# Dense stage of a two-layer graph attention kernel: statistics two groups ahead, normalising and moving in turn on ScalarE, a PSUM wait per tile, edge table stored in 14 pieces

## The reference

```python
h = relu(layernorm(x))                       # per row: (x - mean) / sqrt(var + 1e-5)
for W, a_s, a_d, b in ((W0, ...), (W1, ...)):
    h = (h @ W).reshape(n, 4, 64)
    e = leaky_relu((h * a_s).sum(-1)[src] + (h * a_d).sum(-1)[dst], 0.2)   # with a loop on each node
    alpha = segment_softmax(e, dst)
    h = gelu(segment_sum(h[src] * alpha[:, :, None], dst).reshape(n, 256) + b)
out = x + h
```

## Time and profile before

| | us |
|---|---|
| median of 3 runs (4950.52, 4977.21, 4978.08) | 4977.21 |
| profiled execution, its own time | 4959.4 |
| its span in the trace | 4957.5 |
| first store of a dense group issued | 24.3 |
| last store of the dense stage issued | 166.8 |
| first gather of layer 0 | 169.8 |
| DVE begins the first step of layer 0 | 226.7 |
| POOL, PE, DVE, ACT busy over the span | 3054.6, 2920.6, 3692.9, 2353.5 |

### The profile page before, as it was taken

The page is one execution under the profiler, slowest core; times in us unless marked ns, Lnnn a source line. Parts: engine busy times, 40 slices in busy tenths (PEclk is TensorE's granted clock), DMA queues, the critical chain, the costliest instruction groups (busy, mean ns, idle before and its releaser), DMA issues.

```text
span 4957.5 us, 58322 instructions
## 1 busy us (share of the span) xinstructions
PE 2920.6 (59%) x10195; PEld 1927.3 (39%) x10195; DVE 3692.9 (74%) x13203; ACT 2353.5 (47%) x7376; POOL 3054.6 (62%) x3215
## 2 busy tenths in 40 slices
PE   7467666677666555565545555555555555555555
PEld 6244444444444333343423333333333333333333
DVE  7577777878777677676757777777777777777777
ACT  5255555555555444444443444444444444444445
POOL 7566656666656655566546666666666666666664
PEclk9688888888788777777767777777777777777777
DMA  8444444444444444444434444444444444444443
GB/s 266 141 129 128 128 119 128 132 128 126 125 120 127 124 115 123 117 121 122 122 99 124 128 133 133 133 133 132 133 135 133 132 130 133 133 133 131 134 135 91
DMA packets 326730, 645.75 MB, mean 130 GB/s; under 512 B 97683, under 2 KB 195387, under 8 KB 326635
## 3 DMA queue, kind: packets, MB, share of 16 engines
q0 software_dynamic: 152224, 428.76, 32.5%
q1 hardware_dynamic: 128664, 172.56, 11.5%
q10 hardware_dynamic: 45746, 43.56, 2.6%
HBM read 596.90 MB, written 47.71 MB: 130 GB/s over the span
## 4 chain that ended last, share of the span: by engine, by line
DVE 70%; issue 14%; another core or an unknown queue 11%; PE 2%; ACT 1%; DVEq 1%; POOL 1%; DMA 0%; ACTq 0%; SPq 0%; POOLq 0%
DVE rows_all L1081 9%; DVE groups_or_hots L1106 9%; DVE stores_or_hots L1059 5%; DVE of_node L1162 3%; DVE vectors_or_means L1201 3%; DVE total L1188 3%; DVE node_logit L1160 3%; DVE node_l L1152 2%; DVE runs L1117 2%; DVE dloc L1103 1%; DVE stats_or_carry L1122 1%; DVE runs L1119 1%; DVE logit L1180 1%; DVE pre L1178 1%
## 5 line engine op out<-in xcount | busy, mean ns | idle before, releaser
L598 POOL DMA_INDIRECT rows_all<-table,edge x3068 | 2933.2, 956 | 1821.5 <-issue 953.7
L1328 PE MATMUL bank<-rows_all,groups_or_hots 128*128 128x264 f32 x6272 | 1783.3, 440 | 47.3 <-issue 23.0
L1328 PEld LDWEIGHTS bank<-rows_all,groups_or_hots 128*128 128x128 f32 x6272 | 1328.9, 219 | 452.6 <-issue 147.2
L1310 PE MATMUL bank<-stores_or_hots,logit_p 128*128 128x448 bf16 x896 | 368.8, 566 | 1314.6 <-DVE logit_p L1072 1142.0
L706 ACT ACTIVATE rows_all<-rows_all 128x64 f32<-128x64 f32 x3584 | 881.6, 341 | 3.7
L1310 PEld LDWEIGHTS bank<-stores_or_hots,logit_p 128*128 128x128 bf16 x896 | 98.9, 131 | 1513.0 <-DVE logit_p L1072 1214.7
L1081 DVE TENSOR_TENSOR rows_all<-rows_all,bank 128x768 f32<-128x768 f32 (+1 forms) x672 | 658.8, 1037 | 0.0
L1106 DVE TENSOR_TENSOR groups_or_hots<-bank,dloc 128x1792 f32<-128x1792 f32 x224 | 453.5, 2025 | 159.5 <-remote 101.2
L736 ACT ACT_TABLE_LOAD x224 | 287.4, 1283 | 400.2 <-issue 377.6
L718 ACT ACTIVATE share<-node_d 128x8 f32<-128x8 f32 x224 | 47.0, 210 | 694.5 <-DVE node_d L1155 550.7
L730 ACT ACTIVATE bank<-fall 128x56 f32<-128x56 f32 x224 | 49.6, 222 | 544.2 <-DVE fall L1183 357.8
(11 more groups left out here) (192 smaller groups left out, 4054.9 us busy)
## 6 DMA issues: line engine op xcount, KB each, us to landing
normed_or_dst<-dst_row SPq DMA_DIRECT2D x224, 448.0 KB
rows_all<-table,edge POOLq DMA_INDIRECT x3068
products_or_rows<-table SPq DMA_DIRECT2D x224, 132.0 KB
table<-row ACTq DMA_DIRECT2D x112, 132.0 KB
early_or_lists<-in_x_dram SPq DMA_DIRECT2D x112, 128.0 KB
out_dram<-vectors_or_means ACTq DMA_DIRECT2D x112, 128.0 KB
table<-stores_or_hots ACTq DMA_DIRECT2D x24, 528.0 KB
groups_or_hots<-in_x_dram SPq DMA_DIRECT2D x24, 512.0 KB
```

Source lines behind the costliest of these rows:

```text
L598: nc.gpsimd.indirect_dma_start(out=G[u][:, j, :], out_offset=None, in_=table[L][0:N, :], in_offset=bass.IndirectOffsetOnAxis(ap=index[:, j ...
L1310: last = nc.tensor.matmul(bank[0][:, 0:SLOTS * SQ], logit_p[:, q * P:(q + 1) * P], of[:, q], start=(q == 0), stop=(q == QUADS - 1))
L1328: last = nc.tensor.matmul(bank[3 + t.half][:, 0:ROW], onehot[t.half][:, j, :], G[t.u][:, j, :], start=(j == 0), stop=(j == SLOTS - 1))
```

## The change

DVE: the turn is reordered. The scales of the next group come right behind copy 0, since its statistics were made a turn earlier; the statistics of the group after the next (`later`) are split, two tiles behind copy 0 and two behind copy 1, its sums behind copy 2, and the early tiles behind copies 2 and 3. The first turn makes two groups' statistics. ACT: `norm_group` and `move_rows` are split into tiles that go in turn, and the square root of `later` stands between moves 1 and 2. PE: for an even group it waits for one moved tile of the odd group before instead of four (the semaphore starts at 4 instead of 1 so that the waited value stays positive). POOL: 14 pieces of 640 columns, and so four early gathers behind each.

```diff
-        PIECE = 320
+        PIECE = 640
...
-            def norm_group(g):
+            def deviations(g):
                 m = len(g.sizes)
                 act.wait_ge(mv_done[g.b], g.n + 1)
                 nc.scalar.activation(sdev[g.b][:, 0:m], mv[g.b][:, 0:m, 1], ACT.Sqrt, bias=eps[:, 0:1]).then_inc(sdev_done[g.b], 1)
-                act.wait_ge(shift_done[g.b], g.n + 1)
...
+            def dense_turn(g, after, later):
+
+                norm_tile(after, 0)
+                norm_tile(after, 1)
+                move_tile(g, 0)
+                norm_tile(after, 2)
+                move_tile(g, 1)
+                norm_tile(after, 3)
+                if later:
+                    deviations(later)
+                move_tile(g, 2)
+                move_tile(g, 3)
+                store_group(g)
...
             for j in range(XB):
-                norm_group(Group(0, j + 1))
-                move_rows(Group(0, j))
-                store_group(Group(0, j))
+                dense_turn(Group(0, j), Group(0, j + 1), Group(0, j + 2))
...
-            def between(g, after, early=()):
+            def dense_turn(g, after, later, early=()):
 
                 copy_tile(g, 0)
-                stats_group(after)
+                scales_group(after)
+                if later:
+                    stats_tiles(later, 0, 2)
                 copy_tile(g, 1)
-                scales_group(after)
-                for t in range(2, GROUP):
-                    if early:
-                        early_tile(early[t - 2])
-                    copy_tile(g, t)
+                if later:
+                    stats_tiles(later, 2, GROUP)
+                copy_tile(g, 2)
+                if later:
+                    sums_group(later)
+                if early:
+                    early_tile(early[0])
+                copy_tile(g, 3)
+                if early:
+                    early_tile(early[1])
+
+            def first_turn(g, after, later):
+
+                copy_tile(g, 0)
+                stats_tiles(after, 0, GROUP)
+                sums_group(after)
+                copy_tile(g, 1)
+                scales_group(after)
+                copy_tile(g, 2)
+                stats_tiles(later, 0, GROUP)
+                copy_tile(g, 3)
+                sums_group(later)
...
                 if g.b == 0:
-                    pe.wait_ge(rows_copied[1], g.n * GROUP + 1)
+                    pe.wait_ge(rows_copied[1], g.n * GROUP + (t + 1 - GROUP + ODD_FIRST))
```

More of the change, by code:

```diff
@@ L298, in two_layer_graph_attention @@
         from_one = [normed, hnT_done, rows_done, hnT_copied, rows_copied]
+        ODD_FIRST = GROUP
+        rows_copied_0 = (1, ODD_FIRST)
         block = ctx.enter_context(nc.Block())
@@ L399, in _ @@
                 for each in one:
-                    nc.sync.sem_inc(each, 1)
+                    nc.sync.sem_inc(each, ODD_FIRST if each is rows_copied[1] else 1)
             load_group(Group(0, 0))
@@ L638, in move_rows, with norm_tile @@
-            def move_rows(g):
-                if not isinstance(g.n, int) or g.n > 0:
-                    act.wait_ge(rows_stored[g.b], g.n * 16)
-                for t, r in enumerate(g.sizes):
-                    act.wait_ge(rows_done[t % 2], g.n * GROUP + g.b * GROUP // 2 + t // 2 + 1 + 1)
-                    nc.scalar.activation(row0[g.b][0:r, t, :], bank[3 + t][0:r, 0:ROW], ACT.Identity).then_inc(rows_copied[g.b], 1)
+            def norm_tile(g, t):
+                if t >= len(g.sizes):
+                    return
+                r = g.sizes[t]
+                if t == 0:
+                    act.wait_ge(shift_done[g.b], g.n + 1)
+                    if not isinstance(g.q, int) or g.q > 1:
+                        for k in range(2):
+                            act.wait_ge(hnT_done[k], g.i * (XB // 2 * GROUP) + (g.j // 2 - 1) * GROUP + (g.b + 1) * GROUP // 2 + 1)
+                nc.scalar.activation(hn[g.b][0:r, t, :], xg[g.xb][0:r, t, :], ACT.Relu,
+                                     bias=shift[g.b][0:r, t:t + 1], scale=rstd[g.b][0:r, t:t + 1]).then_inc(normed[g.b], 1)
@@ new lines, in move_tile @@
+            def move_tile(g, t):
+                r = g.sizes[t]
+                if t == 0 and (not isinstance(g.n, int) or g.n > 0):
+                    act.wait_ge(rows_stored[g.b], g.n * 16)
+                act.wait_ge(rows_done[t % 2], g.n * GROUP + g.b * GROUP // 2 + t // 2 + 1 + 1)
+                nc.scalar.activation(row0[g.b][0:r, t, :], bank[3 + t][0:r, 0:ROW], ACT.Identity).then_inc(rows_copied[g.b], 1)
+            def dense_turn(g, after, later):
[10 more added lines that the diff above has]
+                store_group(g)
@@ L646, in store_group @@
             def store_group(g):
-                act.wait_ge(rows_copied[g.b], g.n * GROUP + len(g.sizes) + 1)
+                act.wait_ge(rows_copied[g.b], g.n * GROUP + len(g.sizes) + rows_copied_0[g.b])
                 if not g.last:
@@ L883, in spread_integers, with stats_tiles, sums_group @@
                 return nc.vector.tensor_copy(steps[:, F_HEIR, bass.ds(rounds_ * NB + NB - 1, 1)], no_heir[:])
-            def stats_group(g):
-                dve.wait_ge(x_landed[g.xb], g.turn * 16 + 16 * (2 if g.last else 1))
-                for t, r in enumerate(g.sizes):
+            def stats_tiles(g, t0, t1):
+                if t0 == 0:
+                    dve.wait_ge(x_landed[g.xb], g.turn * 16 + 16 * (2 if g.last else 1))
+                t1 = min(t1, len(g.sizes))
+                for t in range(t0, t1):
+                    r = g.sizes[t]
                     last = nc.vector.bn_stats(stats[g.b][0:r, t, :], xg[g.xb][0:r, t, :])
-                last.then_inc(stats_done[g.b], 1)
+                if t0 < t1 == len(g.sizes):
+                    last.then_inc(stats_done[g.b], 1)
+            def sums_group(g):
                 dve.wait_ge(stats_done[g.b], g.n + 1)
@@ L983, in _ @@
                 logit_columns(0, a).then_inc(w_ext_ready, 1)
-            stats_group(Group(0, 0))
+            stats_tiles(Group(0, 0), 0, GROUP)
+            sums_group(Group(0, 0))
             scales_group(Group(0, 0))
```

63 lines of the change are left out of this document (32 added, 31 removed).

## The result

| | before | after |
|---|---|---|
| median of 10 runs each, us | 4968.09 | 5011.06 |
| lowest to highest, us | 4950.52 to 4994.27 | 4986.59 to 5033.47 |
| ratio after / before | | 1.0081, interval 1.0053 to 1.0109 |
| profiled execution: own time, span, us | 4959.4, 4957.5 | 5033.47, 5031.6 |

The kernel became 0.8% slower, 43 us between the medians: the time lies outside the forecast range, and a slowdown, rival D, is what came. The profiled execution is the highest of its ten, so the difference of the totals is read from the medians, and the trace for where the time goes.

What follows compares the result with a forecast made beforehand. Bound: a chain of waits on DVE, with DVE and PE waiting in turn in the dense stage, then POOL's list. Dense-stage and POOL savings start layer 0 12 us earlier; from a mean of 4966.3, 4954 us; range 4928 to 4988.

Steps and rivals of the forecast that it cites:

- rival D: Dense stage beside the pieces: four gathers in a row delay other engines' instructions; slower, 5000 to 5044 us; chance 0.07.
- DVE's order: Dense stage: cutting up DVE's block removes all 11.4 us of waits for transposes, 126.0 to 114.6 us over 22 groups.
- The first turn: Start of the dense stage: statistics of one group more, once on the path, cost +1.8 us.
- ACT's order: Dense stage: the square root's new place before move 2 and the store holds up nothing; cost 0.
- PE's wait per tile: Dense stage: PE waiting for single moved tiles gives back 0 to 2.3 us; taken as 0.
- SP's loads: Dense stage: x buffers reloaded 2.5 turns ahead instead of 3.5, 13 us of cover instead of 20; cost 0.
- POOL's pieces: POOL's list: 14 fewer pieces at 0.61 us each save 8.5 us, the 12 late gathers ending at 153.2.
- The sum: Dense stage and POOL's list together: first gather of layer 0 at 157.6 or 160.2 us; gain taken as 12 us.
- The tail of 18.4 us: Dense stage's end: last six tiles again take 18.4 us beside back-to-back gathers, ending at 159.1 us; the longer case.
- Carry to the total: Everything behind layer 0's first gather keeps its instructions and starts that much earlier, 12 us off the total.
- Rival B: Dense stage: DMA engines, limited to 334 GB/s, take its gain; 2 to 6 us won, about 4962 us; chance 0.14.
- Rival C: Run into layer 0: DVE's early tiles finish before the pauses, up to 32 us more gained, 4922 us; chance 0.08.

Runs made afterwards that it cites:

- e1: The changed kernel with 28 pieces of 320 columns again, new orders on DVE, ACT and PE kept; 4967.66 us, ratio 0.9981 to the kernel before.
- h4: e1 with PE waiting for all four moved tiles of the odd group before; 4942.7 us, ratio 0.996 to the kernel before.
- h1: The changed kernel with its 56 early gathers replaced by plain loads of 128 consecutive rows, posted by POOL; 4997.82 us in one run.
- f2: e4 plus a POOL pause behind each second gather of the 12 late and first 39 layer-0 gathers; 4934.12 us, ratio 0.9952 to before.
- e4: The changed kernel, 14 pieces of 640 columns, with two short fills on POOL breaking each row of four gathers; 4961.07 us, ratio 0.9965 to before.
- e3: The changed kernel with 28 pieces of 320 columns, two issued in a row and four gathers behind them; 4969.45 us, ratio 0.9972 to before.

## Why the prediction was wrong, step by step

- **DVE's order** (forecast: 126.0 to 114.6): right. e1 has 116.7 for the 22 groups, with the +1.8 of the first turn 116.4 was forecast. DVE's waits for transposes went from 11.4 to 7.0 us, less than the "all of it" that was taken; PE's waits for copies went from 9.0 to 5.5, which was not counted. Two errors met there. This is right for the dense stage; in the total it isn't clear of noise (e1).
- **The first turn** (+1.8): not seen; e1's second store is 4.45 us behind its first.
- **ACT's order** (0): no cost seen; e1's dense stage adds up without one.
- **PE's wait per tile** (0): neither shown nor refuted, see h4.
- **SP's loads** (0, cover of 13 us): right. DVE waited once for rows of x, 0.6 us after, 0.5 before.
- **POOL's pieces** (-8.5 us): this is the step that failed. Its own arithmetic held: a double piece costs 0.58 us, and POOL's pieces and small stores were done at 135.7, some 10 us earlier than in e1 (146.3). But it valued 14 issues by POOL's time alone. They were also the distance between the gathers. Without them the mean distance went from 1.56 to 1.40 us, and the dense stage from 116.7 to 179.1 us. The term was -8.5 us and measured about +50 in the total.
- **The sum.** With the other terms alone e1 gives what this step left: its last groups are stored at 145.1 and 147.1 (forecast 146 and 148), the first gather of layer 0 is at 165.52. Forecast was 157.6 with POOL's 8.5 us; without them 166.1. The two bounds for the landing of POOL's last gather were not both read from rows: the slices of the earlier trace rows show traffic until 168.5 us, not until 166.75, which is when the last store is issued. The 4.4 us taken for this landing and POOL's start came close: e1 has 4.03. The tail of 18.4 us, which the forecast kept as a worse case, did not repeat: in e1 the dense stage is done as POOL's 12 late gathers begin (146.58), so it no longer lies beside gathers at 1.25 us.
- **Carry to the total**: right in kind. The first comparison is 44.8 us late, the median 43; nothing in the steps gave it back.
- **Rival B** (DMA engines): fell. e1 moved up to 336 GB/s in a stretch of 20 us, and its dense stage took the time that was forecast without this limit, and h1 moved 388 GB/s over 20 us. (The demand in it was slightly too high as well: four gathers and a piece, 792 KB in 5.6 us, are 145 GB/s, not 147.) The Trainium skill ("DMA: Bandwidth & Descriptors", Specifications) gives about 358 GB/s as one core's HBM limit; here, with one core at work, the measured 388 is above it and decides.
- **Rival C** (a quicker run into layer 0): not in after, but f2 shows that the room was there, 18.7 us for the early tiles, once the gathers are paced. Of the 27.8 us by which f2's first comparison comes earlier than e4's, 10.7 are left at the sixth, since POOL's paced list is longer.
- **Rival D** (chance 0.07, 5000 to 5044): its time came, 5011, and its sign, the waits in the turns from 60 us on. Its condition, that four in a row are enough, is not what the runs show; in that its number is partly luck. It was derived from rows that showed the effect at a distance of 1.25 us, and was given little weight because "each piece breaks the row". e3 and after itself show what was wrong with that argument: a row of four is nearly harmless if the mean distance stays at 1.57 (e3), and in after the piece between the rows does not protect when the mean falls to 1.40. The forecast's own figures held that mean, 3.12 / 2 before and 5.65 / 4 after. They stood in the text as a saving.

**What stays open** is the mechanism below the pace. Late are the signals of PE to DVE and ACT, and in other stretches short instructions of DVE; the trace gives these waits to nothing it records. How much of the 62 us is lateness and how much is PE's lower clock, which came with it, isn't separated either. A lock between DVE and POOL is an obvious thought: the Trainium skill ("SBUF — State Buffer", on the bandwidth-pool intuition) has a DMA posted by POOL grow from about 620 to 3100 ns beside a DVE copy. The trace here does not agree: from 80 to 100 us POOL needs 0.94 to 0.98 us to post a gather with DVE busy 18.56 of 20 us in e1, and the same (one took 1.13) with DVE busy 5.27 of 20 after, and POOL's list is the one that isn't late. ACT's moves are late as well as DVE's copies, 50.0 and 52.5 us from 60 to 137. No run here separates other paths.

## What to carry to other kernels

An issue that is taken off a queue is also a gap that is taken away: before valuing it by its own duration, work out the mean distance of what remains, and look in the trace of before for a stretch that already runs at that distance. If that stretch shows the other engines' short operations with waits for "issue" or "remote", the saving can turn over. And where such a stretch lies in the main loop, a pause in the unhurried engine's list is worth a trial: here some 0.9 us a step made the kernel 1.6% faster, all of it in one of two layers, for a reason that the runs leave open.

## What was not expected of the hardware

- A graded effect within 0.16 us of distance between indirect gathers: at 1.56 to 1.58 no or 5 us of late signals in the stretch from 60 to 137 us, at 1.48 11.5 us, at 1.40 102.5 us.
- Plain loads from the same queue, four in 2.15 us and 388 GB/s in all, gave none; the 12 indirect gathers behind them in the same run gave 20 us.
- Once PE was kept waiting, its granted clock fell from 1.00 to 0.50 and a group of four matmuls took 2.10 instead of 1.06 us; it came back to 0.99 in the stretch after the gathers ended.
